# Second cross attention: probabilities turned by VectorE and moved by DMAs and GpSimd copies, attended one context later

## What is computed

```
x = x + _L1_xattn_ref(_layernorm(x), ctx_1024, ctx_1024, mask, Wq, bq, Wk, bk, Wv, bv, Wo, bo)

q = _split_heads(query @ Wq + bq)
k = _split_heads(key @ Wk + bk)
v = _split_heads(value @ Wv + bv)
score = jnp.einsum('bhqd,bhkd->bhqk', q, k) / scale
score = score + mask * -1000000000.0
attn = jax.nn.softmax(score, axis=-1)
ctx = jnp.einsum('bhqk,bhkd->bhqd', attn, v)
ctx = ctx.transpose(0, 2, 1, 3).reshape(query.shape[0], -1, D)
return ctx @ Wo + bo
```

## Time and profile before

| | |
|---|---|
| median of three runs | 1242.58 us (1239.2 to 1244.54) |
| profiled execution | 1242.36 us, its span 1241.1 us |
| busy in the span | TensorE 96%, VectorE 59%, ScalarE 42%, GpSimd 11% |
| the stage's loop over contexts | from 402.90 us of the span (first scores round) to 887.43 us (last attended product), 484.5 us |
| all DMA queues | 111,845 packets, 88.21 MB |
| granted TensorE clock, mean | 0.992 |

### The profile page before, as it was taken

How to read it: one execution, slowest core, us unless ns; L and a number is a source line. 1 busy time by engine, 2 the same in 40 slices (tenths; PEclk the granted TensorE clock), 3 DMA queues, 4 the chain that set the end, 5 groups by cost and what they waited for, 6 DMA issues and landing times.

```text
span 1241.1 us, 25508 instructions
## 1 busy us (share of the span) xinstructions
PE 1192.2 (96%) x10841; PEld 884.5 (71%) x10841; DVE 727.4 (59%) x1601; ACT 520.7 (42%) x1028; POOL 141.3 (11%) x164
## 2 busy tenths in 40 slices
PE   7999899989999999999999999999899999999997
PEld 5654377766457777777777777777787667887886
DVE  5456386768683555555545555555686776545732
ACT  3344446843122554545454545454444332222421
POOL 1300022076533000000000000000032100000000
PEclk9999999999999999999999999999899999999999
DMA  9669600200205020111011101001500312222311
GB/s 352 242 232 405 231 1 1 68 10 1 102 18 170 2 103 36 35 36 36 35 36 36 36 35 36 35 36 36 87 2 1 50 28 35 35 34 46 57 34 34
DMA packets 111845, 88.21 MB, mean 71 GB/s; under 512 B 86458, under 2 KB 87532, under 8 KB 107508
## 3 DMA queue, kind: packets, MB, share of 16 engines
q1 hardware_dynamic: 110384, 85.49, 22.1%
q10 hardware_dynamic: 1348, 1.09, 0.3%
HBM read 65.59 MB, written 20.97 MB: 70 GB/s over the span
## 4 chain that ended last, share of the span: by engine, by line
PE 87%; DVE 6%; ACT 3%; DMA 1%; issue 1%; POOL 1%; SPq 0%; POOLq 0%; DVEq 0%; ACTq 0%
PE bank L289 58%; PE bank L245 4%; PE bank L1790 3%; PE bank L559 2%; PE bank L577 2%; PE bank L1811 2%; PE bank L1138 2%; PE bank L1117 2%; DVE W L1380 1%; PE bank L495 1%; PE bank L235 1%; DMA W<-ctx_turned 1%; PE bank L1086 1%; PE bank L1070 1%; PE bank L1094 1%
## 5 line engine op out<-in xcount | busy, mean ns | idle before, releaser
L2023 ACT ACTIVATE W<-W,low 128x512 f32<-128x512 f32 x128 | 91.0, 713 | 57.6 <-DVE low L1929 57.6
L2003 ACT ACTIVATE K<-bank,vecT 128x512 f32<-128x512 f32 x64 | 43.7, 688 | 166.2 <-PE bank L289 166.2
L225 POOL TENSOR_TENSOR rstd<-rstd,half_pow 128x1 f32<-128x1 f32 x48 | 30.8, 644 | 690.6 <-DVE rstd L221 690.6
L1902 DVE TENSOR_TENSOR W<-bank,vecT 128x256 f32<-128x256 f32 x16 | 6.8, 424 | 164.1 <-PE bank L1811 164.1
L1929 DVE CUSTOM_DVE_ANT_0 W<-bank,W 128x512 f32<-128x512 f32 x128 | 80.8, 687 | 30.9 <-PE bank L1790 30.9
L289 PE MATMUL bank<-ctxT,Wkv 128*128 128x512 f32 x384 | 93.6, 396 | 0.7 <-DVE ctxT L306 0.7
L289 PE MATMUL bank<-xT,wT 128*128 128x512 f32 x384 | 92.5, 390 | 0.8 <-ACT W L2860 0.5
L289 PE MATMUL bank<-Wq,Wkv 128*128 128x512 f32 x384 | 93.1, 394 | 0.0
L289 PE MATMUL bank<-Wkv,ctxT 128*128 128x512 f32 x384 | 92.9, 394 | 0.0
L289 PE MATMUL bank<-Wkv,Wq 128*128 128x512 f32 x384 | 92.1, 395 | 0.0
L289 PEld LDWEIGHTS bank<-Wkv,ctxT 128*128 128x128 f32 x384 | 70.8, 188 | 27.2 <-issue 13.0
(11 more groups left out here) (345 smaller groups left out, 2162.0 us busy)
## 6 DMA issues: line engine op xcount, KB each, us to landing
W<-ctx_turned SPq DMA_DIRECT2D x16, 1024.0 KB, 4.9
W<-in_ctx_dram SPq DMA_DIRECT2D x8, 1024.0 KB, 10.3
ctx_turned<-ctxT SPq DMA_DIRECT2D x8, 1024.0 KB, 7.3
ctx_turned<-W SPq DMA_DIRECT2D x8, 1024.0 KB, 6.5
XT<-in_ctx_dram SPq DMA_DIRECT2D x4, 1024.0 KB, 11.8
XT<-in_L_ffn_wi_dram SPq DMA_DIRECT2D x64, 64.0 KB, 2.1
raw_own<-in_ctx_dram SPq DMA_DIRECT2D x3, 1024.0 KB, 10.8
XT<-in_L_ffn_wo_dram SPq DMA_DIRECT2D x48, 64.0 KB, 2.1
```

What stands on the lines that cost most here:

```text
L225: pool.tensor_tensor(rstd[:, g:g + 1], rstd[:, g:g + 1], half_pow[:], ALU.pow).then_inc(rstd_ok.s, 1)
L2003: act.activation(K[:, m, :], bank[:, n % 4, :], ACT.Identity, bias=pcol("L1_xattn_bk", m)).then_inc(ring_a.s, 1)
L2023: act.activation(PR[:, j, :], PR[:, j, :], ACT.Exp, bias=low[:, j:j + 1], scale=-1.0, accum_out=total[:, j:j + 1]).then_inc(expd.s, 1)
```

## The change

The probabilities are no longer turned by TensorE. ScalarE scales each tile by the reciprocal of its total (`scaled_a`; VectorE takes four reciprocals in one instruction, `recips_v`), VectorE turns the 32x32 blocks within the tile (`dve.transpose` in `probs_v`), and the 16 blocks of partitions by strips are then put in place in `PT`: the 12 that change partitions by DMAs from SP (`move_probs`, 32 partitions x 16 pieces of 32 numbers each), and the four that stay on their partitions by GpSimd copies. This is done for each half of the tiles. The attended product of context i is computed in context i + 1, behind its second scores round; so the values lie in two places by turns (`values`, the second is weight slot 3), and `PT` is written once the attended product before has read it. The output product moves from behind value product 1 to behind the second key tile. The next stage's key weight is loaded into `V`, between the last two halves' moves, and turned at the very end.

```diff
             for i in range(NI):
-                USES += [("value", i, k) for k in range(2)]
+                USES += [("value", i, 0)]
+                if i:
+                    USES += [("attended", i - 1, 0)]
+                USES += [("value", i, k) for k in range(1, KT)]
+                if i < NI - 1:
+                    USES += [("key", i + 1, m) for m in range(2)]
                 if i and i % 2 == 0:
                     USES += [("output", i // 2 - 1, 0)]
-                USES += [("value", i, k) for k in range(2, KT)]
                 if i < NI - 1:
-                    USES += [("key", i + 1, m) for m in range(C)]
-                    USES += [("attended", i, 0)]
+                    USES += [("key", i + 1, m) for m in range(2, C)]
...
+            values = (V[:], slot(3))
...
+            def probs_landed(engine, i, half):
+                engine.wait_ge(pt_in[half].s, pt_in[half](12 * i + 11))
+                engine.wait_ge(kept_p.s, kept_p(8 * i + 4 * half + 3))
+
+            def block_of(i, half, q, r):
+                pairs, strip, to = slice(4 * half, 4 * half + 4), slice(32 * r, 32 * r + 32), slice(32 * q, 32 * q + 32)
+                return (PT[strip, pairs, :, to].rearrange("p t k n -> p (t k) n"),
+                        PR[to, pairs, :].rearrange("p t (k n) -> p (t k) n", n=P)[:, :, strip])
+
+            def move_probs(i, half):
+
+                sp.wait_ge(probs.s, probs(XPAIRS * i + 4 * half + 3))
+                if i:
+                    sp.wait_ge(ring.s, ring(use_of["attended", i - 1, 0]))
+                for q in range(4):
+                    for r in range(4):
+                        if q != r:
+                            there, here = block_of(i, half, q, r)
+                            sp.dma_start(there, here).then_inc(pt_in[half].s, 16)
...
-                sp.wait_ge(wt_v.s, wt_v(0))
-                load_slot(3, "L1_attn_Wk")
-                for i in range(1, NI - 1):
-                    sp.wait_ge(ctx_v.s, ctx_v(4 * i + 3))
-                    load_context(i + 1)
-                sp.wait_ge(ctx_v.s, ctx_v(4 * (NI - 1) + 3))
-                load_slot(4, "L1_attn_Wv")
-                sp.wait_ge(pt_pe.s, pt_pe(2 * NI - 1))
+                for i in range(NI):
+                    move_probs(i, 0)
+                    if i < NI - 1:
+                        sp.wait_ge(ctx_v.s, ctx_v(4 * (i + 1) + 3))
+                        if i < NI - 2:
+                            load_context(i + 2)
+                        else:
+                            load_slot(4, "L1_attn_Wv")
+                    else:
+                        sp.dma_start(V[:], a["L1_attn_Wk"].rearrange("(c p) n -> p c n", p=P)).then_inc(slot_in[3].s, 16)
+                    move_probs(i, 1)
+                for half in range(2):
+                    probs_landed(sp, NI - 1, half)
                 load_slot(5, "L1_attn_Wq")
 
             def gpsimd():
...
+                for i in range(NI):
+                    for half in range(2):
+                        pool.wait_ge(probs.s, probs(XPAIRS * i + 4 * half + 3))
+                        if i:
+                            pool.wait_ge(ring.s, ring(use_of["attended", i - 1, 0]))
+                        for q in range(4):
+                            there, here = block_of(i, half, q, q)
+                            pool.tensor_copy(there, here).then_inc(kept_p.s, 1)
+                        pool.wait_ge(kept_p.s, kept_p(8 * i + 4 * half + 3))
+                    if i == 0:
+                        pool.wait_ge(row_in.s, row_in())
+                        for j in range(G):
+                            pool.wait_ge(x_in[j].s, x_in[j]())
+                            pool.tensor_tensor(X[:, j, :], X[:, j, :], bias_row, ALU.add).then_inc(biased.s, 1)
...
+                    if i and i % 2 == 0:
+                        row_stats_pool(4, i // 2 - 1)
...
                 elif i:
-                    pe.wait_ge(pt_a.s, pt_a(XPAIRS * i - 1))
+                    pe.wait_ge(lowest.s, lowest(XPAIRS * i - 1))
...
             def attend_pe(i):
                 b = free_bank("attended", i, 0) if i < NI - 1 else bank[:, 4, :]
                 taken_pe("value", i, KT - 1)
-                pe.wait_ge(pt_a.s, pt_a(XPAIRS * i + XPAIRS - 1))
+                for half in range(2):
+                    probs_landed(pe, i, half)
...
                     scores_pe(i, 1)
+                    if i:
+                        attend_pe(i - 1)
                     values_pe(i, 1)
-                    if i and i % 2 == 0:
-                        output_pe(i // 2 - 1)
                     if not more:
                         value_weight_pe()
                     values_pe(i, 2)
                     values_pe(i, 3)
                     if more:
-                        keys_pe(i + 1, 0)
-                    probs_pe(i, 0)
+                        for m in range(2):
+                            keys_pe(i + 1, m)
+                    if i and i % 2 == 0:
+                        output_pe(i // 2 - 1)
                     if more:
-                        keys_pe(i + 1, 1)
-                        keys_pe(i + 1, 2)
-                    else:
-                        key_weight_pe()
-                    probs_pe(i, 4)
-                    if more:
-                        keys_pe(i + 1, 3)
-                    else:
-                        for g in range(3):
-                            pe.wait_ge(pt_a.s, pt_a(XPAIRS * i + 5 + g))
-                            transpose_rows(xn5, 4, g, 5 + g)
-                    attend_pe(i)
+                        for m in range(2, C):
+                            keys_pe(i + 1, m)
+                pe.wait_ge(wt_v.s, wt_v(4))
+                for g in range(3):
+                    transpose_rows(xn5, 4, g, 5 + g)
+                key_weight_pe()
+                attend_pe(NI - 1)
...
             def scores_v(i, j):
                 dve.wait_ge(score.s, score(2 * i + j // 4))
-                if i:
-                    dve.wait_ge(pt_pe.s, pt_pe(2 * (i - 1) + j // 4))
+                if i and j % 4 == 0:
+                    probs_landed(dve, i - 1, j // 4)
...
+            def recips_v(i, half):
+                dve.wait_ge(expd.s, expd(XPAIRS * i + 4 * half + 3))
+                dve.reciprocal(total[:, 4 * half:4 * half + 4], total[:, 4 * half:4 * half + 4]).then_inc(recip.s, 1)
+
             def probs_v(i, j):
-                dve.wait_ge(expd.s, expd(XPAIRS * i + j))
-                dve.reciprocal(total[:, j:j + 1], total[:, j:j + 1]).then_inc(recip.s, 1)
-                dve.wait_ge(recip.s, recip(XPAIRS * i + j))
-                dve.tensor_scalar(PR[:, j, :], PR[:, j, :], total[:, j:j + 1], None, ALU.mult).then_inc(probs.s, 1)
+
+                dve.wait_ge(scaled_p.s, scaled_p(XPAIRS * i + j))
+                dve.transpose(PR[:, j, :], PR[:, j, :]).then_inc(probs.s, 1)
...
+            def scaled_a(i, half):
+                act.wait_ge(recip.s, recip(2 * i + half))
+                for t in range(4 * half, 4 * half + 4):
+                    act.mul(PR[:, t, :], PR[:, t, :], total[:, t:t + 1]).then_inc(scaled_p.s, 1)
```

More of the change, by code:

```diff
@@ L1959, in vector @@
                         scores_v(i, t)
-                    if j is not None:
-                        halves_v(j)
+                    recips_v(i, 0)
                     for t in range(4, XPAIRS):
                         scores_v(i, t)
+                    for t in range(4):
+                        probs_v(i, t)
+                    recips_v(i, 1)
                     value_v(i, 0)
+                    if i:
+                        attended_v(i - 1)
                     value_v(i, 1)
-                    if j is not None:
-                        output_v(j)
                     for r in range(4):
@@ L1972, in vector @@
                             value_weight_v(r)
-                    for t in range(4):
-                        probs_v(i, t)
-                    if j is not None:
-                        dve.wait_ge(xsum.s, xsum(3 * G + j))
-                        row_stats_v(j)
-                    value_v(i, 2)
-                    if not more:
-                        value_v(i, 3)
                     for t in range(4, XPAIRS):
@@ L1983, in vector @@
                     if j is not None:
-                        normalise(xn5, 4, j)
-                    if more:
-                        value_v(i, 3)
-                    else:
-                        for r in range(4):
-                            key_weight_v(r)
-                    attended_v(i)
+                        halves_v(j)
+                    value_v(i, 2)
+                    value_v(i, 3)
+                    if j is not None:
+                        output_v(j)
+                        dve.wait_ge(xsum.s, xsum(3 * G + j))
+                        row_stats_v(j)
+                    elif i > 1:
+                        normalise(xn5, 4, i // 2 - 1)
                     if i == 0:
@@ L1993, in vector @@
```

(41 more changed lines are left out.)

33 lines of the change are left out of this document (8 added, 25 removed).

## The result

The changed kernel took 1205.94 us (median of 4 runs, 1204.93 to 1210.99) where the kernel before took 1243.36 (4 runs, 1239.2 to 1244.54): 0.9709 of it, interval 0.9687 to 0.9732. In a second comparison it was 1210.24 (6 runs) against 1241.24, 0.9738 (0.9707 to 0.9769). Forecast were 1205.6 and a range of 1196 to 1234. The profiled execution is the slowest of the first four, 1210.99 us with a span of 1209.7.

What follows compares the result with a forecast made beforehand. The prediction took TensorE, busy 96% of the span, as the bound. Its terms, -3.2 - 5.2 - 37.6 + 5.6 + 3.6 = -36.8 us, took 1242.4 to 1205.6, with a range of 1196 to 1234.

Steps and rivals of the forecast that it cites:

- context 0: First context: no attended product and no turns, but key 0 waits for the split until 14.8; 25.7 us, saves 3.2.
- contexts 2 to 14, with their waits: Seven even contexts at 28.94 us and six odd at 26.22: 359.9 against 397.51, saves 37.6 before split waits.
- last context: Final context: TensorE waits for half 1's moves behind the key weight's load; 30.3 us to its product's end, costs 3.6.
- What TensorE loses: TensorE in each context: two turns of 1.12 us and 0.53 more go; new even context 28.94, odd 26.22.
- split waits: TensorE waiting on VectorE's split of the next context beside GpSimd's copies: 0.4 us a context, 14 times, costs 5.6.
- The cover of 0.3 us: Slack between VectorE's split of the next context ending at T+15.0 and TensorE starting key 0 at T+15.34; the thinnest.
- GpSimd's copies: Four copies of 32x512 from T+10.3, taken at 0.8 us each, lasting until 13.5, 1.0 us into the splits.
- The rival with 1.26: GpSimd's copies near 1.26 us outlast the splits and cost 2.6 a context: 1236 us; shares chance 0.18 with dearer moves.
- A move at 0.53 us: SP's price for each DMA, taken from the last stage: 12 moves take 6.3 us, half 1 lands at 26 to 28.
- The cover of 3 to 5 us: Slack between half 1's moves landing at 26 to 28 and their being wanted at T+31.3 at the earliest.
- the rival of 0.7 to 0.8 a move: At 0.8 us a move half 1 lands 2.2 late in odd contexts: 1221 us; shares chance 0.18 with dear copies.
- the slower rival: A move out of SBUF costs 1.06 us, twice the DRAM one; contexts follow the moves, about 1290 us; chance 0.14.

Runs made afterwards that it cites:

- copies_short: Changed kernel with each GpSimd copy cut to a sixteenth from context 1 on, leaving most diagonal blocks unmoved: 1202.16 us in one run.
- same_context: Changed kernel with the attended product put back into its own context, behind the last key tile: 1296.51 us.
- out_early: Changed kernel with the output product behind value product 3 again, ahead of the next context's first two key tiles: 1236.41 us.
- copies_twice: Changed kernel with each GpSimd copy made twice: 1220.88 us.
- wk_first: Changed kernel with the key weight's load issued ahead of all 24 moves in the last context: 1204.27 us.
- wk_first_two_queues: Changed kernel with the key weight's load ahead of the last context's moves and six of the last twelve moves issued by ScalarE: 1202.88 us.
- last_by_pe: Changed kernel, key weight's load ahead of the last context's moves, that context's last half turned by TensorE and copied by ScalarE: 1191.73 us.

## Why the prediction was right

| term | forecast | measured | how |
|---|---|---|---|
| context 0 | -3.2 | -2.8 | 28.93 to 26.17 |
| context 1, with its split wait | -4.8 | -5.1 | 31.42 to 26.30 |
| contexts 2 to 14, with their waits | -32.4 | -34.6 | 397.51 to 362.95 |
| last context | +3.6 | +7.9 | 26.67 to 34.61 |
| sum | -36.8 | -34.5 | 484.53 to 450.03 |

The mechanism was right, and the sum is right to 2.3 us. That the median lies 0.3 from the forecast is partly luck: two terms are wrong by 2.2 and 4.3 and stand against each other, and the changed kernel's own two medians are 4 apart, 37.4 and 31.0 us below the kernel before.

*What TensorE loses* held to the hundredth. copies_short runs at the forecast 26.22 and 28.94. With the copies it is 26.30 and 29.02.

*Contexts 2 to 14*: thirteen contexts of the forecast come to 359.9, and 0.08 more in each makes 360.9. Two gaps of 0.68 and 1.02 us inside an attended product, in contexts 5 and 6, which the trace gives to no releaser ("issue"), bring it to 362.6. They are no accident of one run: in ten profiles (all but those of the kernel before, same_context, out_early and copies_twice) context 5 takes 27.1 to 27.6 us and context 6 29.9 to 30.5. Their cause is open. Such stray time stood in the earlier trace rows too: 397.51 is 2.8 more than seven contexts of 31.62 and six of 28.90, nearly all of it in contexts 7 and 8 (29.52 and 33.57). The forecast set a clean sum against one with strays, which flattered the gain by some 2; its split waits were too high by 4.2, and the 2.2 of the table are the difference.

*The cover of 0.3 us* was mis-sized, and with it the split waits: 5.6 forecast, 1.1 measured (14 x 0.08). Two sizes were off. A wait of 0.4 us behind a cover of 0.3 means splits that take 0.7 longer beside the copies; they take 0.42 longer (2.90 against 2.48), since only the last copy meets one. And the split started at T+12.15, not 12.5. I had put the four VectorE instructions ahead of it (reciprocal, value copy, attended sum, value copy) at 1.9 us, nearly their full durations, where from one start to the next they take 1.6 (721.00 to 722.60). That made the cover 0.6, and the 0.42 fit inside it.

The mechanism, a split that waits for GpSimd to end, is what the traces show. In copies_twice three of the four splits meet a copy and take 1.10 us instead of 0.68. The copy that started at 730.62 ends at 731.67 and the split beside it at 732.22, 0.54 later; the next copy, from 731.73, ends at 732.69, 0.48 after that split; and so on to the last split. So the two engines take turns, each waiting until the other's instruction is over, and each meeting costs a split 0.42. The Trainium skill ("SBUF — State Buffer", section Who interferes with whom) has the other engine blocked for a whole instruction, and the trace agrees.

*GpSimd's copies*: 0.8 forecast. The median is 0.61 when VectorE leaves them alone (2.69 for four); the mean of 0.70 on the page holds those that waited for a split. The rival with 1.26 fell with this.

*A move at 0.53 us* failed: 0.67, and 0.78 in the second half, behind the context load (9.33 for 12), where one issue of the twelve takes 1.98 us. Half 1 was to land at 26 to 28 and lands at 30.5. The cover of 3 to 5 us is 0.8. It cost nothing in contexts 0 to 14, but the rival of 0.7 to 0.8 a move was much nearer than its place in the forecast says: SP sends 24 moves in a row, so 0.8 us are used up by 0.03 more for each, at 0.71 us a move.

*The last context* was 4.3 us off (30.3 forecast, 34.6). It is the same step: with half 0 out only at T+18.3, the load goes at T+18.4 (forecast 16.9), half 1 at T+19.1 to 29.3 (forecast 17.5 to 23.8), and the product starts at T+31.0 instead of 27.5. 3.5 us are this, and the other 0.8 are the product at the low clock, 3.64 where I took 2.8. wk_first, wk_first_two_queues and last_by_pe show it: 32.8, 28.6 and 23.1 as the load goes first, the issues are shared and the last half's are left out.

*Context 0* was 0.5 off. The end of its chain of waits (start, us, what):

```profile
417.69 2.96 DVE Wq L306 x4
420.64 0.14 issue
420.78 11.13 PE bank L289 x48
```

Key 0 starts at T+15.1 instead of 14.8, for the four splits take 2.96 us here, 0.47 more than the 2.49 they were priced at. The key tiles then take 11.06 to the next scores instead of 10.88.

Of the slower rival the runs show the mechanism, not its price: in same_context the attended product waits for its moves, because the context of delay is gone, at 0.67 a move.

## What to carry to other kernels

Work taken off the bound engine is worth its start-to-start distance, and a slow way round it (here 30 us through three engines and a queue) costs next to nothing (0.08 us a context here) as long as a whole iteration lies between; in the last iteration nothing lies there, so keep the short way for it. Count the issues of a queue end to end, not each batch against its own deadline: 24 issues in a row turn 0.14 us each into 3.4. When an engine's chain decides a cover of a few tenths, use distances between starts for each instruction, not durations.

## What was not expected of the hardware

- Behind a wait of 2.77 us at the same place, the granted clock fell in some contexts and not in others (0.95 and 1.00 over the context, 33.50 and 32.00 us). That kernel spreads over 16.4 us in 10 runs, the kernel before over 10.5 in the 15 beside them (1235.66 to 1246.19), wk_first over 4.6 in 5.
- SP's issue of a 64 KB DMA in 128 B pieces took 0.67 us in this stage, from SBUF or DRAM, to a scattered or a dense destination and in either order, and 0.52 in the last stage of the same execution.
- A VectorE instruction with two SBUF inputs and a GpSimd copy beside it wait for each other in turns. The split that met a copy took 1.10 us instead of 0.68, the copy 0.96 to 1.05 instead of 0.61; a split whose copies were over took 0.68 again. So what counts is how many copies the splits still meet: one in the changed kernel (0.42 us), three in copies_twice (1.25).
- SP's issue of a context's 1 MB load took 0.32 us in the kernel before and 0.62 in the changed one.
